# Cross attention: VectorE norms the rows two tiles ahead in front of the last tile's residual instead of behind it

## What is computed

```
def layernorm(x, eps=1e-05):
    m = jnp.mean(x, axis=-1, keepdims=True)
    v = jnp.var(x, axis=-1, keepdims=True)
    return (x - m) / jnp.sqrt(v + eps)

def xattn(q, kv, seg_id, W_kvc, W_dq, W_uq, W_qr, W_uk, W_kr, W_uv, W_o):   # 16 heads
    kv_c, q_c = kv @ W_kvc, q @ W_dq                  # compressed, 64 and 96 wide
    q_nope, q_rope = q_c @ W_uq, rope(q_c @ W_qr)
    k_nope, v, k_rope = kv_c @ W_uk, kv_c @ W_uv, rope(kv_c @ W_kr)
    scores = (q_nope . k_nope + q_rope . k_rope) / sqrt(192)
    scores = where(seg_id - 8 <= key <= seg_id, scores, -1e30)
    return softmax(scores) @ v @ W_o

x = x + xattn(layernorm(x), ctx_2048, itok_BxS_0_1023, ...)
x = x + self_attention(layernorm(x), ...)
x = x + mixture_of_experts(layernorm(x), ...)
```

## Time and profile before

| | |
|---|---|
| median of 3 runs | 528.61 us (528.29 to 529.51) |
| profiled execution, its own time | 530.75 us |
| its span, first to last instruction | 528.9 us |
| TensorE busy | 504.2 us, 95% of the span |
| VectorE busy | 253.0 us, 48% |
| ScalarE busy | 186.3 us, 35% |
| GpSimd busy | 60.5 us, 11% |
| TensorE's share of the chain that ended last | 83% |
| granted TensorE clock, mean | 0.987 of full speed |

### The profile page before, as it was taken

How to read it: one execution, slowest core, us unless ns; L and a number is a source line. 1 busy time by engine, 2 the same in 40 slices (tenths; PEclk the granted TensorE clock), 3 DMA queues, 4 the chain that set the end, 5 groups by cost and what they waited for, 6 DMA issues and landing times.

```text
span 528.9 us, 10582 instructions
## 1 busy us (share of the span) xinstructions
PE 504.2 (95%) x3876; PEld 364.0 (69%) x3876; DVE 253.0 (48%) x549; ACT 186.3 (35%) x533; POOL 60.5 (11%) x71
## 2 busy tenths in 40 slices
PE   8989999999999979998899999899999999999997
PEld 6566776767767768886688887455555555556886
DVE  3765765866856657989644221222222222222235
ACT  2266566556567524444331111221121121121110
POOL 2000000000000012223103520000000000000650
PEclk9898999999999989999999999999999999999999
DMA  9700000000892005900162235488778778762231
GB/s 301 293 20 4 18 21 0 20 20 0 292 422 100 2 5 193 403 4 0 22 280 90 79 108 213 148 300 299 269 285 307 270 276 316 266 244 71 84 119 47
DMA packets 24459, 82.08 MB, mean 155 GB/s; under 512 B 2881, under 2 KB 16513, under 8 KB 20322
## 3 DMA queue, kind: packets, MB, share of 16 engines
q1 hardware_dynamic: 21536, 75.93, 39.5%
q0 software_dynamic: 1536, 4.20, 2.5%
q10 hardware_dynamic: 1346, 1.38, 0.8%
HBM read 73.11 MB, written 8.39 MB: 154 GB/s over the span
## 4 chain that ended last, share of the span: by engine, by line
PE 83%; DVE 7%; issue 5%; ACT 2%; DMA 2%; DVEq 1%; SPq 0%; POOL 0%; ACTq 0%; POOLq 0%
PE ps L1790 17%; PE ps L1703 12%; PE ps L1307 10%; PE ps L1814 9%; PE ps L1715 6%; PE ps L1386 5%; PE ps L1336 5%; PE ps L1355 5%; PE ps L1470 3%; PE ps L1374 2%; DMA w_routed<-in_w_qr 2%; PE ps L1328 1%; ACT w_routed L1086 1%; PE ps L1480 1%; PE ps L1659 1%
## 5 line engine op out<-in xcount | busy, mean ns | idle before, releaser
L1790 PE MATMUL ps<-w_routed,xnT 128*64 x320 | 93.8, 436 | 1.6 <-DVE x_sb L956 1.6
L1703 PE MATMUL ps<-xT_all,w_shared 128*128 128x256 f32 x320 | 75.7, 380 | 0.0
L1790 PEld LDWEIGHTS ps<-w_routed,xnT 128*64 128x64 f32 x320 | 42.0, 137 | 38.4 <-issue 27.2
L1703 PEld LDWEIGHTS ps<-xT_all,w_shared 128*128 128x128 f32 x320 | 60.3, 190 | 8.4 <-issue 0.4
L1086 ACT ACTIVATE w_routed<-ps,neg_top 128x128 f32<-128x128 f32 x128 | 45.1, 379 | 19.4 <-DVE neg_top L626 19.4
L1307 PEld LDWEIGHTS ps<-consts_a,w_routed 128*128 128x128 f32 x336 | 38.2, 144 | 19.6 <-issue 16.1
L1307 PE MATMUL ps<-consts_a,w_routed 128*128 128x128 f32 x336 | 46.4, 282 | 5.2 <-DVE w_routed L614 1.8
L1814 PE MATMUL ps<-w_routed,hidT 128*64 x200 | 47.4, 384 | 0.0
L1790 PE MATMUL ps<-x_up,xnT 128*64 128x384 f32 (+1 forms) x160 | 46.9, 436 | 0.0
L1790 PE MATMUL ps<-w_shared,xnT 128*64 128x384 f32 (+1 forms) x160 | 46.9, 436 | 0.0
L1249 ACT ACTIVATE sil<-ps 128x256 f32<-128x256 f32 x40 | 15.3, 384 | 84.7 <-PE ps L1703 60.6
(11 more groups left out here) (180 smaller groups left out, 877.0 us busy)
## 6 DMA issues: line engine op xcount, KB each, us to landing
w_routed<-in_w_routed SPq DMA_DIRECT2D x8, 1920.0 KB, 14.5
x_up<-in_w_routed SPq DMA_DIRECT2D x10, 1280.0 KB, 6.0
w_shared<-in_w_routed SPq DMA_DIRECT2D x10, 1280.0 KB, 5.9
b_down<-in_w_routed SPq DMA_DIRECT2D x10, 640.0 KB
w_shared<-in_w_routed SPq DMA_DIRECT2D x10, 640.0 KB, 5.7
w_shared<-in_w_shared SPq DMA_DIRECT2D x1, 3840.0 KB, 12.1
w_shared<-in_w_uvo SPq DMA_DIRECT2D x1, 2560.0 KB, 15.6
x_slots<-sil SPq DMA_DIRECT2D x16, 160.0 KB, 2.2
```

What stands on the lines that cost most here:

```text
L1703: last = pe.matmul(ps[:, UP_BANK[m], half_ * D:(half_ + 1) * D].rearrange("p (n t) -> p n t", n=2), w_shared[:, j, at:at + P], xT_all[:, i ...
L1790: last = pe.matmul(ps[rows, b, 0:hi - lo], xnT[:, k, rows], w, start=k == 0, stop=k == KT - 1)
```

## The change

`normed` leaves the head of VectorE's `body` and stands behind `front_qt`, in front of the residual, for the tile two ahead. The number that it waits for is the same for each tile. `normed(1)`, which was the head of `body(0)`, is now written out ahead of it; `normed(8)` doesn't exist, hence `if more`.

```diff
--- before.py
+++ after.py
@@ -673,7 +673,6 @@
                 b_queries(1)
 
             def body(i, link_, behind, more):
-                normed(i + 1, (2, 3)[i] if isinstance(i, int) and i < 2 else 2 * i, xn, xT_ps, xn_ready, i + 1)
                 maxima(i, 0)
                 query_compressed(i + 1)
                 if more:
@@ -688,6 +687,8 @@
                 front_rotated(i + 1)
                 divided(i, 1, link_)
                 front_qt(i + 1)
+                if more:
+                    normed(i + 2, 3 if isinstance(i, int) and i == 0 else 2 * i + 2, xn, xT_ps, xn_ready, i + 2)
                 if behind:
                     residual(i - 1, link_)
 
@@ -715,6 +716,7 @@
 
             front_qt(0)
             dve.wait_ge(x_in, 16)
+            normed(1, 2, xn, xT_ps, xn_ready, 1)
             body(0, link, False, True)
             body(1, link, True, True)
             base = steps[0]
```

## The result

The changed kernel takes 522.94 us (median of 4, 522.19 to 524.61) against 529.06 us (528.29 to 529.66) before: ratio 0.9889, 95% interval 0.9859 to 0.9920, 6.1 us less. The forecast was 522.2, range 520.5 to 524.8. The profiled execution took 524.61, its span is 522.7 us against 528.9.

What follows compares the result with a forecast made beforehand. TensorE was taken to bound the cross attention, stalled at five edges for xn behind VectorE's residual and loop edge. With 0.41 us of work moved, 0 added and 6.4 us of stall gone: 528.6 - 6.4 = 522.2 us, range 520.5 to 524.8.

Steps and rivals of the forecast that it cites:

- What bounds: Cross attention: TensorE sets the pace and at tile edges waits for xn, behind VectorE's residual and loop edge.
- The main term: Five edges, probs_T to scores: 12.13 us before less 5 x 1.14 = 5.70 needed, so 6.4 us gained.
- (a) to (c): All stalls go, 522.2, chance 0.74; new wait keeps part, 523.4 (far end 527.5), 0.12; clock changes, 520.5 or 523.9, 0.08.
- The waits view's 4.9: TensorE's listed wait for xn from VectorE, 4.9 us in five times, kept as low bound of the gain.
- xn 1.0 us early: At a tile edge, xn is ready for TensorE at 84.27, 1.0 us ahead of probs_T being through at 85.27.
- x2_done spare 1.2 us: The later residual raises x2_done 0.41 us later, still 1.2 us before the second half of the scores wants it.
- ut_out 0.4: ScalarE's ut_out ends 0.4 us before the first half of the scores wants it.
- VectorE's loop edge: Now ahead of the first maximum: spare 0.35 us, the smallest cover; beyond it each 0.1 us returns four times at most.
- TensorE's loop edge at price 0: Branch at four of five edges costs nothing once the xn wait goes; other bound: only the first edge's 1.14 us gained.
- Rival (e), slower: Norm held by GpSimd's rstd delays x2_done: costs from 1.2 us, slower than before from 2.7 us; chance 0.02.
- Rival (c), the clock: Clock drop between 190 and 200 us, more or less, moves time about 1.7 us: 520.5 or 523.9; chance 0.08.
- the prediction's own signs of being wrong: New TensorE waits at L1351 or L1097, "issue" idle of some tenths at its loop edge, or longer stages behind 190 us.

Runs made afterwards that it cites:

- n1: Changed kernel with the norm still at the end of body but behind the residual's five instructions: 527.75 us, ratio to before 0.9979.
- n2: Changed kernel with the norm inside the residual, behind the sum that raises x2_done and in front of bn_aggr: 525.16 us, ratio to before 0.9916.
- n6: Changed kernel with a VectorE filler reduction of 128x1800 in front of the norm, behind front_qt: 529.44 us, ratio to before 0.9987.
- n5: Changed kernel with a VectorE filler reduction of 128x1800 between the norm and the residual: 527.10 us, ratio to before 0.9966.
- n4: Changed kernel with a VectorE filler reduction of 128x1800 behind the residual at each of the five edges: 524.38 us, ratio to before 0.9913.
- n7: Changed kernel with a longer VectorE filler reduction, 128x3000, behind the residual: 531.50 us, ratio to before 1.0027.
- n0: The changed kernel timed once more without an edit, against the kernel before: 523.40 us, ratio 0.9883.

## Why the prediction was right, and where it was not

- **What bounds.** That the edge hung on VectorE's residual and loop edge is shown: n1 puts the residual back and loses 4.35 us, n2 puts back three of its five instructions and loses 1.76, and n6 puts in their place a filler of 1.93 us, which loses 5.2 of the 6.4 us by the trace; its median can't be told from before.
- **The main term.** 12.13 - 5.70 = 6.4 us; measured 6.38 in the trace and 6.1 and 6.2 in the medians. The 524.6 under the range has no term of its own: by their numbers (a) to (c) end at 523.9. The waits view's 4.9 would have been too low, and n2 shows why: a wait of 0.22 us and a slow start of 0.13 appear in it as nothing.
- **xn 1.0 us early, x2_done spare 1.2 us, ut_out 0.4.** The first two were forecast with 0.14 us off for TensorE's start. Measured in the same terms they are 1.17 - 0.14 = 1.03 and 1.24 - 0.14 = 1.10, and `ut_out` 0.45. n5 confirms the second by its price: 1.93 of filler cost 0.76, so 1.17 was covered.
- **VectorE's loop edge.** Two errors. Its spare was given as 0.35 us, by taking all 0.76 us between L556 and the norm as the edge. Where the maximum comes behind it, the edge is 0.44 (L557 at 84.76 to L627 at 85.20 in n5), so 83.67 + 0.44 = 84.11 against 84.88 left 0.77. For the same reason VectorE's idle time before the first maximum is 1.05 us and not the few tenths of the forecast. And "each 0.1 us would come back" is wrong: in n4 the first maximum was 0.80 us late and 0.23 was lost, in n7 2.06 late and 1.51 lost. TensorE meets the maxima again at `y_lat`, by way of VectorE's own order, and at `y_rope`, by way of the exponentials and the keys' copy; the second is the tighter, with 0.55 us of cover. So this cover was not the smallest: it is 0.77 + 0.55 = 1.3 us, and the smallest by the trace is `ut_out`'s 0.45, which no run tested. The 1.7 us that n4 and n7 show are these 1.3 and the loop's edge, which costs nothing behind the filler. The forecast stood because both errors only understated the cover.
- **TensorE's loop edge at price 0.** Right: 0.93 us between the transposes at the branch, 1.15 at all five stretches, whether loop entry or loop edge. The stall that the prediction drew from the Trainium skill's rule on taken branches ("Runtime: NRT & Kernel Launch", "Instruction fetch mechanics") shows at none of the five. At the edge shown, the branch came 2.5 us ahead of the matmuls; what it costs TensorE without such a lead, no run shows.
- **Rival (e), slower.** Its place was right, its arithmetic was not. It put the price at 1.2 us of holding, by `x2_done`, and the break-even with before at 2.7. A held norm makes `xn` late first, which had 1.03 us to spare. n6, held 1.93 us, lost 1.03 at each edge, with the wait at `xn`. The gain is 6.4 / 5 = 1.28 an edge, so the break-even lies at some 2.2 us by an estimate from these numbers.
- **Rival (c), the clock.** It did move: 3.2 us lost in the ten behind the cross attention instead of 1.7 in the profiled executions. With it one of the prediction's own signs of being wrong came true, the stages behind the cross attention took 1.0 us longer. It doesn't make the gain: in n0's profile the same ten were granted 0.83, as before the change, and the ratio was the same. Whether the shift by 6 us moved the clock or the executions merely differ isn't shown. That the median's gain is 6.1 and 6.2 and not 6.4 is inside the interval.

## What to carry to other kernels

An instruction that is ready long before must not stand behind work that its consumer doesn't need, and a loop's edge counts as such work: on VectorE it took 0.44 us or more behind a short instruction. Price such a stall start to start against the same sequence where it isn't waited for, not by the idle time shown. Before calling a spare the smallest, follow what is delayed to the next instruction on the bounding engine that really waits for it.

## What the runs showed of the hardware that was not expected

- A loop's edge on VectorE was free behind a long instruction: in n4 the maxima start 1.93 us after the start of the filler, with no idle time, although the loop's edge lies between; behind the short last step of the residual it showed as idle time (0.28 us in n5).
- A TensorE that had to wait is slow to start: from the two transposes of `xn` to the scores it took 0.22 us unwaited, and 0.33 to 0.41 behind a wait, even one of which no idle time is shown (n2: 84.03 to 84.38).
- Times of one kernel went with its mean granted clock: of the changed kernel's four runs, the two at 0.993 took 522.19 and 522.31, the two at 0.986 took 523.58 and 524.61.
